# In 15 of 64 units the second state is scanned into SBUF and weighed by GpSimd: a hybrid block of attention, feed-forward and state-space layers

## The reference

```
x = x + attention(layernorm(x))        # 16 heads, latent of 32, rotary, causal
x = x + ffn(layernorm(x))              # weights and activations quantized to blockwise FP4
x = x + mamba(layernorm(x))            # two directions, d_inner 512, 16 states
x = x + ffn(layernorm(x))
```

```
dA  = exp(dt * A);  dBu = dt * B_ssm * xc
h_t = dA_t * h_(t-1) + dBu_t           # over the 512 positions
y_t = sum over the 16 states of h_t * C_t   (then + xc * D_skip)
```

## Time and profile before

| | before |
|---|---|
| median of 3 executions | 4327.49 us (4325.34 to 4328.36) |
| the profiled execution | 4323.4 us, span 4321.6 us |
| granted TensorE clock, mean of the span | 0.943 |
| TensorE busy | 3528.9 us, 82% |
| VectorE busy | 3215.6 us, 74% |
| ScalarE busy | 1959.6 us, 45% |
| GpSimd busy | 1925.1 us, 45%, 1122 instructions |
| DMA | 649.65 MB, mean 150 GB/s |

### The profile page before, as it was taken

One profiled execution on the slowest core, in us unless ns is written; L12 is line 12 of the kernel. 1 busy time (PEld: TensorE's weight loads), 2 busy tenths in 40 slices (PEclk: granted clock), 3 DMA queues, 4 the chain that ended last, 5 costly groups with the idle time before them and its releaser, 6 DMA issues.

```text
span 4321.6 us, 41545 instructions
## 1 busy us (share of the span) xinstructions
PE 3528.9 (82%) x13488; PEld 1876.9 (43%) x13488; DVE 3215.6 (74%) x4556; ACT 1959.6 (45%) x3692; POOL 1925.1 (45%) x1122
## 2 busy tenths in 40 slices
PE   5885897789978898879987899788988799878657
PEld 5552454245543454434543455434544345434214
DVE  3243778977688867978688776878679787887994
ACT  0343464534645355534645346353555346553441
POOL 0201643536444454445544464444544445443770
PEclk9997999999999899999999999998999999999998
DMA  3002543744436344363435444363453644354780
GB/s 82 1 1 84 183 149 122 250 155 153 147 129 238 123 141 161 132 227 129 157 125 204 158 154 143 125 238 131 139 164 123 235 129 152 127 197 161 253 281 8
DMA packets 203817, 649.65 MB, mean 150 GB/s; under 512 B 34253, under 2 KB 45520, under 8 KB 197456
## 3 DMA queue, kind: packets, MB, share of 16 engines
q1 hardware_dynamic: 203600, 646.98, 44.8%
HBM read 595.52 MB, written 51.38 MB: 150 GB/s over the span
## 4 chain that ended last, share of the span: by engine, by line
PE 46%; DVE 21%; issue 18%; ACT 9%; POOL 5%; SPq 1%; DMA 1%; DVEq 0%; POOLq 0%; ACTq 0%
PE banks L1257 17%; PE banks L1501 9%; DVE banks L864 7%; PE banks L1438 6%; PE banks L1286 5%; PE banks L1262 5%; DVE sb_arena L871 4%; ACT banks L1223 4%; PE banks L1414 3%; POOL sb_arena L991 3%; DVE sb_arena L792 2%; ACT sb_arena L1028 2%; DVE sb_arena L617 2%; SPq L426 1%; ACT sb_arena L1092 1%
## 5 line engine op out<-in xcount | busy, mean ns | idle before, releaser
L991 POOL TENSOR_TENSOR sb_arena<-sb_arena 128x1024 f32<-128x1024 f32 x512 | 1213.2, 2371 | 871.6 <-PE banks L1501 592.6
L864 DVE TENSOR_TENSOR_SCAN banks<-banks,sb_arena 128x512 f32<-128x512 f32 x1024 | 1198.1, 1215 | 181.7 <-ACT banks L1223 135.0
L1501 PE MATMUL banks<-sb_arena,sb_ident 128*128 128x512 f32 x2048 | 1042.4, 637 | 336.9 <-DVE sb_arena L871 268.2
L1223 ACT ACTIVATE banks<-sb_arena,sb_neg_a 128x512 f32<-128x512 f32 x1024 | 665.4, 682 | 1249.9 <-DVE sb_arena L871 1243.8
L1501 PEld LDWEIGHTS banks<-sb_arena,sb_ident 128*128 128x128 f32 x2048 | 384.6, 200 | 821.0 <-DVE sb_arena L871 430.2
L1028 ACT ACTIVATE sb_arena<-banks 128x512 f32<-128x512 f32 (+4 forms) x752 | 381.1, 519 | 636.4 <-PE banks L1262 447.4
L871 DVE TENSOR_TENSOR sb_arena<-banks,sb_arena 128x512 f32<-128x512 f32 x1024 | 651.1, 677 | 0.0
L1262 PE MATMUL banks<-sb_ident,sb_arena 128*128 128x128 f32 (+1 forms) x2082 | 355.7, 295 | 312.9 <-ACT sb_arena L1028 86.1
L1262 PEld LDWEIGHTS banks<-sb_ident,sb_arena 128*128 128x128 f32 (+1 forms) x2082 | 252.1, 149 | 531.4 <-ACT sb_arena L1028 156.6
L737 DVE TENSOR_REDUCE sb_nmax<-banks 128x1 f32<-128x512 f32 (+3 forms) x352 | 223.2, 637 | 285.6 <-PE banks L1441 284.2
L1257 PE MATMUL banks<-sb_w_gu,sb_arena 128*128 128x352 f32 x1024 | 347.1, 487 | 14.0 <-ACT sb_arena L1028 14.0
(11 more groups left out here) (127 smaller groups left out, 4097.3 us busy)
## 6 DMA issues: line engine op xcount, KB each, us to landing
sb_arena<-rows_bc SPq DMA_DIRECT2D x1024, 512.0 KB, 4.4
kept_xc<-sb_arena SPq DMA_DIRECT2D x16, 1024.0 KB, 4.9
kept_z<-sb_arena SPq DMA_DIRECT2D x16, 1024.0 KB, 4.5
sb_arena<-kept_z SPq DMA_DIRECT2D x64, 256.0 KB, 5.0
sb_arena<-kept_xc SPq DMA_DIRECT2D x64, 256.0 KB, 4.6
kept_zs<-sb_arena SPq DMA_DIRECT2D x8, 1024.0 KB, 6.6
sb_arena<-kept_zs SPq DMA_DIRECT2D x8, 1024.0 KB, 9.5
sb_xin<-in_x SPq DMA_DIRECT2D x8, 512.0 KB, 7.4
```

The lines of the kernel that those rows point to most:

```text
L864: v.tensor_tensor_scan(factors, factors, products, 0.0, ALU.mult, ALU.add).then_inc(V.sem, V.mark("scan", K, e))
L991: nc.gpsimd.tensor_tensor(dBu[K % SLOTS], u[:, p % 2].unsqueeze(1).to_broadcast([P, 2, T]), rows_b[K % BS], ALU.mult).then_inc(G.sem, G.ma ...
L1223: nc.scalar.activation(psum[:, e], dt[:, (K // NQ) % 2], ACT.Exp, scale=neg_a[:, s, m, 2 * q + e:2 * q + e + 1]).then_inc(A.sem, A.mark("d ...
L1501: mm = pe.matmul(psum[:, YB], ident[:, :], dBu[K % SLOTS][:, e], start=(q == 0 and e == 0), stop=(q == NQ - 1 and e == 1))
```

## The change

In the units SHARED of each batch, 5, 7, 9, 11 and the odd ones from 43 to 63, 15 of 64 (120 of 512 in all), the scan of the second state writes over its own products in `dBu`, in SBUF. VectorE multiplies the first state alone; GpSimd multiplies the second, in place, in a new step `weigh_state`, which stands after `make_dBu(K + 2)` and ahead of its first visit. The waits follow: TensorE's sum and SyncE's next rows of C wait for GpSimd's multiply too, and ScalarE may write the second bank as soon as the scan has read it. The set ADDED is empty, so that what belongs to it is never run. In each part of the diff the context is cut.

```diff
+ADDED, SHARED = (), (5, 7, 9, 11) + tuple(range(43, NU, 2))
...
+        def shared(K):
+            return K % NU in SHARED
...
-                if K >= CS:
+                if K >= CS and shared(K - CS):
+                    sp.wait_ge(V.sem, V.at("hc", K - CS, 0))
+                    sp.wait_ge(G.sem, G.at("hc", K - CS))
+                elif K >= CS:
                     sp.wait_ge(V.sem, V.at("hc", K - CS, 1))
...
-                        v.tensor_tensor_scan(factors, factors, products, 0.0, ALU.mult, ALU.add
-                                             ).then_inc(V.sem, V.mark("scan", K, e))
+                        v.tensor_tensor_scan(products if e == 1 and shared(K) else factors, factors, products, 0.0,
+                                             ALU.mult, ALU.add).then_inc(V.sem, V.mark("scan", K, e))
                     advance(side, visits[2 * k])
-                    for e in range(2):
+                    for e in range(1 if shared(K) else 2):
...
+            def weigh_state(K):
+                g.wait_ge(V.sem, V.at("scan", K, 1))
+                g.wait_ge(s_c[K % CS], 16 * (K // CS + 1))
+                nc.gpsimd.tensor_tensor(dBu[K % SLOTS][:, 1], dBu[K % SLOTS][:, 1], rows_c[K % CS][:, 1], ALU.mult
+                                        ).then_inc(G.sem, G.mark("hc", K))
...
                     if K + 2 < NK:
                         make_dBu(K + 2)
+                    if shared(K):
+                        weigh_state(K)
                     advance(side, visits[2 * k])
...
-                if K >= 1:
+                if K >= 1 and e == 1 and shared(K - 1):
+                    a.wait_ge(V.sem, V.at("scan", K - 1, e))
+                elif K >= 1:
                     a.wait_ge(V.sem, V.at("hc", K - 1, e))
...
+                for e in range(last + 1):
+                    if e == 1 and shared(K):
+                        pe.wait_ge(G.sem, G.at("hc", K))
+                    elif not added(K):
+                        pe.wait_ge(V.sem, V.at("hc", K, e))
                     mm = pe.matmul(psum[:, YB], ident[:, :], dBu[K % SLOTS][:, e],
```

More of the change, by code:

```diff
@@ L396, in unit, with added @@
             return b, p, q, p // DT, p % DT
+        def added(K):
+            return K % NU in ADDED
+        def shared(K):
+            return K % NU in SHARED
         def tile_at(t):
@@ L992, in make_dBu, with add_states @@
                                         ALU.mult).then_inc(G.sem, G.mark("dBu", K))
+            def weigh_state(K):
[3 more added lines that the diff above has]
+                                        ).then_inc(G.sem, G.mark("hc", K))
+            def add_states(K):
+                g.wait_ge(V.sem, V.at("hc", K, 1))
+                nc.gpsimd.tensor_tensor(dBu[K % SLOTS][:, 0], dBu[K % SLOTS][:, 0], dBu[K % SLOTS][:, 1], ALU.add
+                                        ).then_inc(G.sem, G.mark("pair", K))
             for i in range(3 * CK):
@@ L1013, in _ @@
                         make_dBu(K + 2)
+                    if shared(K):
+                        weigh_state(K)
                     advance(side, visits[2 * k])
+                    if added(K):
+                        add_states(K)
                     if p + 1 < NG:
@@ L1498, in state_sum @@
                     pe.wait_ge(V.sem, V.at("ycat", g - 1))
-                for e in range(2):
-                    pe.wait_ge(V.sem, V.at("hc", K, e))
+                if added(K):
+                    pe.wait_ge(G.sem, G.at("pair", K))
+                last = 0 if added(K) else 1
+                for e in range(last + 1):
[3 more added lines that the diff above has]
+                        pe.wait_ge(V.sem, V.at("hc", K, e))
                     mm = pe.matmul(psum[:, YB], ident[:, :], dBu[K % SLOTS][:, e],
-                                   start=(q == 0 and e == 0), stop=(q == NQ - 1 and e == 1))
+                                   start=(q == 0 and e == 0), stop=(q == NQ - 1 and e == last))
                 mm.then_inc(E.sem, E.mark("summed", K))
```

## The result

| | before | after |
|---|---|---|
| median | 4327.34 us | 4373.11 us (4370.66 to 4375.65) |
| ratio to before, 95% interval | | 1.0106 (1.0089 to 1.0124) |
| span of the profiled execution | 4321.6 us | 4370.8 us |
| granted TensorE clock, mean of the span | 0.943 | 0.928 |
| VectorE busy | 3215.6 us | 3165.8 us |

The kernel became slower by 45.8 us, 1.06%. The forecast was 35 us slower. The medians here are of four executions each.

What follows compares the result with a forecast made beforehand. It took the loop scan, scan, L871, ScalarE's exponential as the bound, the second L871 hidden. Batches 1 to 6 at 5.15 us plus batches 0 and 7 gave 35.1; 4323.4 + 35.1 + 4.1 = 4362.6, said 4363 us, range 4310 to 4388.

Steps and rivals of the forecast that it cites:

- Step 1: Unit 63 and TensorE behind it: GpSimd's late last multiply delays the sum and the batch, +2.2 us, lower bound 1.3.
- Steps 2 and 5: Unit 5: GpSimd's multiply blocks VectorE's small instructions, +1.2 us; unit 43: it delays L575, +0.9 us.
- Rival A: Faster: VectorE keeps the right of way over GpSimd's multiply, so the blocking losses go; 4307 us, chance 0.13.
- Step 3: Units 7, 9, 45 and 47: whatever is saved or lost falls into VectorE's next wait for TensorE; 0.
- step 7: Units 55 to 61: no effect, 0, with GpSimd having up to 29.3 us of work per 30 us group.
- Step 4: Units 11 and 12: GpSimd's work moves by 1.27 us, so the four L617 also meet L974; +1.1 us, bounds 0.4 and 1.3.
- Step 6: Units 49 to 53: freed L780 sums -3.95 us, twelve L792 rows +2.3, unit 53 +1.4; together -0.25, from -3.3 to +2.
- Rival C: GpSimd's order becomes the bound: late L991 or C rows cost each batch's last two groups 2 us more; 4400 us, chance 0.08.

Runs made afterwards that it cites:

- the wait alone: The kernel before, all multiplies on VectorE, with one wait added: in unit 49 GpSimd waits for VectorE's second scan before its statistics; 4313.72 us, ratio 0.9973.
- the changed kernel with the three waits: The changed kernel plus GpSimd waits before q, k, x preparation, before units 48 and 49's statistics, and before building the next batch's states; 4298.44 us, ratio 0.9924.
- the two waits alone: The kernel before, with GpSimd waiting for the latent's norm before q, k, x preparation and for normed x before units 48 and 49's statistics; 4261.04 us, ratio 0.9855.

## Why the prediction was right, and where it was not

**Sign and size.** 35 us forecast, 45.8 measured. Nine of the ten rows of the table have the sign that they were given, or are within 0.2 us of nothing where nothing was said; of the seven priced terms four are within 0.15 us of their size, two are off by 0.5 and one by 0.7. What the prediction said that the profile would show is there: GpSimd busy 157 us more (152), VectorE less than 78 less, three of the four sums short, the twelve conv rows over 15 us, the row L587 of unit 43 (L575 before) at 1.47 us (1.6). The table's sizes are from the profiled executions, whose spans differ by 49.2 us, 3.4 more than the medians.

**Step 1** (unit 63): right in mechanism and size in the changed kernel, +2.2 for +2.2, all of it GpSimd's late multiply. The sum ends 4.2 us behind the only L883 of unit 63 (L871 before), as promised. For the one multiply alone the step had 1.3 us as its lower bound; alone it measured 0.7 us of waiting and 1.5 of TensorE's clock, and the clock is in no step.

**Steps 2 and 5** (units 5 and 43): right, 1.07 for 1.2 and 0.82 for 0.9. Rival A, VectorE keeping the right of way, is dead: the multiply starts 0.04 us before L613 and holds it. The write in place of the multiply shows that the reads do it.

**Step 3 and step 7's units 55 to 61**: right in the sum. Eight of these units shared cost and gained nothing on balance; the 0.8 us that units 0 and 1 lost there, and the 0.6 that unit 7 won, are not in the steps. In batch 7 of the changed kernel units 56 and 63 are 0.8 and 0.7 us longer, where the steps had 0 and 0.5; I have not traced it.

**Step 4** (unit 12): right place, wrong size, 0.42 for 1.1. The four L617 took 4.82 us for 4.39, where I had them meet L974 in full. It was my lower bound.

**Step 6**: all three parts right in place, with sizes -4.4 for -3.95, +2.8 for +2.3 and +1.4 for +1.4; the sum is -0.2 for -0.25, partly because the first two errors cancel. That the relief is GpSimd's order is shown by the wait alone, which gains 11 us without any shared unit. What I read off and stopped at was a defect of the kernel before.

**What was missed** is unit 54, 3.0 x 6 = 18 us. Step 6 counted what unit 53 costs VectorE and took the next units to be as before; it did not ask how long TensorE then idles and at which clock it comes back. Without it the forecast would have been too high: 35.1 against 49.2 - 18 = 31 by the spans, about the 0.7 x 6 = 4 that step 4 had too much, and against 45.8 - 18 = 28 by the medians. So some of the closeness is luck, two errors against each other. The question was in reach, since the profile of before has the idle stretches and the clock of each; the size was not, since the same idle stretch of 1.40 us went with either clock.

**Rival C** (GpSimd's order becomes the bound) did not show: the scans wait 44.5 us for GpSimd's make_dBu, 46.4 before, and units 55 to 63 are as long as they were.

## What to carry to other kernels

Busy shares did not decide here: 42 us taken off VectorE in eight units changed nothing in the total, because the loop hung on another engine. GpSimd work that reads SBUF is not free beside VectorE even when GpSimd is idle half of the time; ask what it stands beside, and try a wait that moves it under the scans (or other rows with one SBUF operand) before moving work to it. And where a stage grows longer by a microsecond, look at how long TensorE idles in it: the granted clock of the stage behind can cost more than the stage.

## What I had not expected of the hardware

- Half clock was one of the largest terms of the loss, 2.4 us a batch in unit 54 beside 2.2 for GpSimd's late multiply of unit 63. The four dt products took 1.98 us at 1.00 and 3.78 at 0.50; with unit 49 alone shared, unit 54 took 6.54 us in one batch and 8.36 to 9.15 in the other five of one and the same run.
- Whether the clock falls can hang on work far ahead: units 5 and 43 shared left unit 54 long in four batches and as before in two, the changed kernel had it long in all six, and the changed kernel with the three waits in none. No run here tells what sets the batches apart: with the two waits alone, batches 2 and 3 both idled 1.40 us ahead of the dt products, and one went on at 0.50 and the other at 1.00.
- A GpSimd write of 128x512 (0.52 us) didn't touch VectorE's 128x4 rows beside it; a multiply of the same tile holds such a row of 0.16 us for 1.24.
